# Cross attention: mask widened ahead of the context split, scores issued in pairs on 64 rows each

## The reference, cut to what matters

```
x: 32 x 100 x 256, context: 32 x 361 x 256, mask: 32 x 100 x 361 (bool)
Q = LN(x) Wq + bq;  K = ctx Wk + bk;  V = ctx Wv + bv      16 heads of 16 channels
scores = where(mask, Q K / sqrt(16), lowest float);  A = softmax(scores) V
x = x + tanh(g0) * (A Wo + bo)
x = x + tanh(g1) * experts_attention(LN(x))                8 heads x 8 experts
```

## Time and profile before

| what | value |
|---|---|
| median of 3 runs | 2058.17 us (2057.41 to 2060.99) |
| profiled execution, its own time | 2054.61 us |
| its span, first to last instruction | 2053.0 us |
| busy PE / PEld / DVE / ACT / POOL | 1911.7 / 1177.6 / 1497.5 / 1141.0 / 930.7 us |
| mean granted TensorE clock | 0.970 |

### The profile page before, as it was taken

How to read it: one execution, slowest core, us unless ns; L and a number is a source line. 1 busy time by engine, 2 the same in 40 slices (tenths; PEclk the granted TensorE clock), 3 DMA queues, 4 the chain that set the end, 5 groups by cost and what they waited for, 6 DMA issues and landing times. The chain is left out here.

```text
span 2053.0 us, 59140 instructions
## 1 busy us (share of the span) xinstructions
PE 1911.7 (93%) x13454; PEld 1177.6 (57%) x13454; DVE 1497.5 (73%) x4285; ACT 1141.0 (56%) x3588; POOL 930.7 (45%) x1361
## 2 busy tenths in 40 slices
PE   5788899899889799999999999968999999999998
PEld 2577777777777555444444444436555555555553
DVE  6477777778778795255555555556999999999989
ACT  3477777777778644444444444434555555555543
POOL 3112112211221200266666666653766666767767
PEclk9899999999999899999999999987999999999999
DMA  3676776677666248200000000034222222222201
GB/s 115 120 102 99 103 104 101 104 100 110 100 105 88 82 199 318 124 26 26 26 26 26 26 26 26 26 107 149 83 71 75 76 73 75 71 75 70 84 14 64
DMA packets 192135, 174.07 MB, mean 85 GB/s; under 512 B 51921, under 2 KB 183378, under 8 KB 190034
## 3 DMA queue, kind: packets, MB, share of 16 engines
q1 hardware_dynamic: 189906, 165.06, 35.6%
q0 software_dynamic: 2176, 8.39, 1.2%
HBM read 112.41 MB, written 60.98 MB: 84 GB/s over the span
## 5 line engine op out<-in xcount | busy, mean ns | idle before, releaser
L1343 POOL TENSOR_TENSOR o_side<-o_side,o_tmp 128x256 f32 (+1 forms) x528 | 397.5, 753 | 193.3 <-POOL o_side L1343 73.5
L1069 ACT ACTIVATE big<-e_pv,gates 128x128 f32<-128x128 f32 x800 | 228.0, 368 | 292.1 <-PE e_pv L1131 290.6
L609 ACT ACTIVATE c_ex<-c_sm,c_nmax 100x361 f32<-100x361 f32 x512 | 302.6, 593 | 122.5 <-DVE c_nmax L499 109.6
L499 DVE CUSTOM_DVE_ANT_0 c_sm<-c_ps,c_mbias 100x361 f32<-100x361 f32 x512 | 269.3, 527 | 118.4 <-PE c_ps L687 59.4
L1464 ACT ACTIVATE o_tmp<-o_py,gates 128x256 f32<-128x256 f32 x528 | 221.9, 474 | 192.0 <-PE o_py L1537 141.8
L1131 PE MATMUL e_pv<-e_vhi,e_xhi 128*128 x800 | 303.2, 379 | 1.2 <-ACT e_out L1059 1.2
L1537 PE MATMUL o_py<-o_whi,a_chi 128*128 128x512 f16 x800 | 303.7, 380 | 0.6 <-DVE o_side L1397 0.3
L1131 PE MATMUL e_pv<-e_vlo,e_xhi 128*128 x800 | 303.2, 379 | 0.0
L1131 PE MATMUL e_pv<-e_vhi,e_xlo 128*128 x800 | 303.2, 379 | 0.0
L1537 PE MATMUL o_py<-o_whi,a_clo 128*128 128x512 f16 x800 | 303.1, 379 | 0.0
L1537 PE MATMUL o_py<-o_wlo,a_chi 128*128 128x512 f16 x800 | 303.0, 379 | 0.0
(11 more groups left out here) (166 smaller groups left out, 3401.3 us busy)
## 6 DMA issues: line engine op xcount, KB each, us to landing
qk<-e_out SPq DMA_DIRECT2D x16, 1600.0 KB, 5.2
c_kst<-k_parts SPq DMA_DIRECT2D x256, 90.2 KB, 4.9
v<-e_out SPq DMA_DIRECT2D x20, 640.0 KB, 3.3
a_q<-qk SPq DMA_DIRECT2D x64, 200.0 KB, 2.5
a_k<-qk SPq DMA_DIRECT2D x64, 200.0 KB, 2.4
a_v<-v SPq DMA_DIRECT2D x64, 200.0 KB
c_ctx<-in_ctx_t SPq DMA_DIRECT2D x32, 361.0 KB, 3.4
e_wst<-in_v_w POOLq DMA_DIRECT2D x8, 1024.0 KB, 8.1
```

Of the source, the lines that this page charges most:

```text
L499: dve.tensor_tensor_reduce(out=sm[:, h % 4, :], in0=p_s[0:SQ, h % 2, 0:SK], in1=mbias[:, b.par, :], scale=-0.25 / WS, scalar=BIG, op0=ALU. ...
L609: act.activation(ex[:, h % 4, 0:SK], sm[:, h % 4, :], ACT.Exp, scale=-1.0, bias=nmax[:, h % 4:h % 4 + 1], accum_out=den[:, b.par, HEAD[h]: ...
L1069: act.activation(tmp[:, hh, e, :], p_v[:, hh, 1, e * PD:(e + 1) * PD], ACT.Copy, scale=gate).then_inc(s_av, 1)
L1343: pool.tensor_tensor(side[:, x.t, :], side[:, x.t, :], tmp[:, slot(x, r), j, :], ALU.add).then_inc(s_pool, 1)
```

## The change

It reorders POOL (mask of the next batch ahead of the split, first mask and split ahead of the wait for `s_tg`), gives each scores matmul only the 64 rows that hold its head, issues the scores of two heads together in even steps, reorders `HEAD` so that each two neighbours are an even and an odd head, and lets DVE copy two heads behind every second mask. The accumulation flags of `attend` follow the group of four in place of the parity of the head.

```diff
-HEAD = (0, 2, 4, 6, 1, 3, 5, 7, 8, 10, 12, 14, 9, 11, 13, 15)
+HEAD = (0, 3, 4, 7, 1, 2, 5, 6, 8, 11, 12, 15, 9, 10, 13, 14)
...
-                pool.wait_ge(s_tg, 1)
-
-                def body(b):
+
+                def widen_mask(b):
                     pool.wait_ge(s_mask[b.par], 16 * (b.half + 1))
                     at_least(pool, s_sm, XH * (b.n - 1))
                     pass_wait(pool, s_pass_pool)
                     pool.tensor_scalar(mbias[:, b.par, :], mraw[:, b.par, :], BIG, -BIG,
                                        ALU.mult, ALU.add).then_inc(s_mb, 1)
+
+                def bias_x(b):
                     pool.wait_ge(s_x[b.par], 16 * (b.half + 1))
                     at_least(pool, s_x1, b.n - 1)
                     pool.tensor_tensor(xbias[:, b.par, :], xb[:, b.par, :], tgbo[0:SQ, :],
                                        ALU.add).then_inc(s_xb, 1)
+
+                def body(b):
+                    bias_x(b)
+                    if later(b, 1):
+                        widen_mask(later(b, 1))
                     if later(b, 3):
                         split(later(b, 3))
 
+                widen_mask(fixed(0))
                 split(fixed(2))
+                pool.wait_ge(s_tg, 1)
                 batches(pool, body)
...
                     for i in range(XH):
-                        lagging(b, i, LAG_C, copy_ext)
                         masked(b, i)
+                        if i % 2 == 1:
+                            lagging(b, i, LAG_C, copy_ext)
+                            lagging(b, i, LAG_C - 1, copy_ext)
...
-                for i in range(XH, XH + LAG_C):
-                    lagging(last, i, LAG_C, copy_ext)
+                for h in range(XH - LAG_C + 1, XH):
+                    copy_ext(last, h)
...
-                    pe.matmul(p_s[0:SQ, h % 2, 0:SK], qst[:, b.par, HEAD[h], :], kst[:, b.par, HEAD[h] // 2, :],
+                    row = P // 2 * (HEAD[h] % 2)
+                    pe.matmul(p_s[0:SQ, h % 2, 0:SK], qst[row:row + P // 2, b.par, HEAD[h], :],
+                              kst[row:row + P // 2, b.par, HEAD[h] // 2, :],
                               start=True, stop=True).then_inc(s_s, 1)
...
-                                             start=odd == 0 and c == 0, stop=odd == 1 and c == KC - 1)
+                                             start=first // CLOSE % 2 == 0 and c == 0,
+                                             stop=first // CLOSE % 2 == 1 and c == KC - 1)
...
                     for i in range(XH):
-                        scores(b, i)
+                        if i % 2 == 0:
+                            scores(b, i)
+                            scores(b, i + 1)
```

## The result

| | before | after |
|---|---|---|
| median | 2059.11 us (4 runs, 2057.41 to 2060.99) | 2037.19 us (4 runs, 2034.08 to 2038.59) |
| ratio of the runs | | 0.9891, 95% interval 0.9874 to 0.9908 |
| profiled execution / its span | 2054.61 / 2053.0 us | 2037.69 / 2036.1 us |
| mean granted TensorE clock | 0.970 | 0.976 |

Faster by 22 us (1.1%), where 44 were forecast: the sign was right, the size was half, and the time lies inside the range of 1975 to 2046.

What follows compares the result with a forecast made beforehand. The late mask on POOL was taken to stall DVE and PE, with PE pacing otherwise. Batches go from 18.73 to 16.16 + 0.96 = 17.12 us: 46.7 gained less 2.9, net 43.8, forecast 2014 us, range 1975 to 2046.

Steps and rivals of the forecast that it cites:

- mask ahead of the split: POOL's order: DVE's wait and PE's lowered clock go, 18.73 to 16.16 us per batch, 74.5 us over 29 batches.
- early second score, copies in twos: PE and DVE order within a batch: taken as zero, PE having 2.1 us per pair, DVE needing 1.8.
- halved rows: shape changes less overlap: PE's score pairs: 0.44 us against 0.32 through drains at shape changes, +0.96 us per batch.
- batch 0: First batch: gains no mask wait and pays 0.96 us for its pairs.
- batches 30, 31 and later stages: Last batches: 30 and 31 gain no mask wait and each pay 0.96 us for pairs.
- the 1984 that the prediction has for it: Whole-kernel time in us if a pair of scores costs just what two scores did before.
- The bound that I gave for the late copies alone: DVE's copies of heads 3, 5, 9, 11: at most 4 x 0.464 = 1.86 us per batch on PE's path.
- The second rival: DVE's late copies hold PE: two of four arrive on its path, batch 18.05 us, 2044 us; chance 0.13.
- My own sign of failure: Working fails if PE idles on `c_nmax` or `c_ext` over 1 us per batch: pair cost then does not pace PE.
- The pairs do not gain (1965, 1984): Rival on PE's scores: row halves switch without drain, 1965 us, or pairs cost nothing extra, 1984; chance 0.18.
- the tiles within a pair do not drain against each other (2084): Rival: the lower-to-upper tile step drains too, pair 0.71 us, batch 19.28, 2084 us; chance 0.07.
- The mask does not come last: Rival on the mask's DMA: landing some 5 us after issue, the wait stays, 2058 us; chance 0.06.

Runs made afterwards that it cites:

- mask_only: The kernel before with nothing but POOL's new order (next batch's mask ahead of the split): 1987.4 us, ratio 0.9637.
- pairs_128: The kernel after, but every score multiplies all 128 rows again; order, HEAD and copies as changed: 2007.4 us, ratio 0.9735.
- single_64: mask_only with each score on its own 64 rows, one at a time in the old order: 2092.5 us, ratio 1.0147.
- batch0_128: The kernel after with all 128 rows in batch 0 alone: 2031.1 us, ratio 0.9880.
- pairs_same_rows: The kernel after with the old HEAD list, so both scores of a pair lie on the same 64 rows: 2066.2 us, ratio 1.0010.
- first_64: mask_only with halved rows in batch 0 alone, one score at a time: 1996.3 us, ratio 0.9706.
- pairs_only: The kernel after with POOL's old order: 2148.8 us, ratio 1.0441.

## Why the prediction was right or wrong, point by point

Against the forecast's own base, the profiled execution, the change gave 2054.6 - 2037.7 = 16.9 us and not 43.8. Over the 29 batches from the second to the thirtieth (mean lengths from first mask to first mask; mask_only 16.34, pairs_128 17.15):

| term | forecast us | measured us |
|---|---|---|
| mask ahead of the split | +74.5 | 29 x (18.73 - 16.34) = +69.3 |
| early second score, copies in twos | 0 | 29 x (16.34 - 17.15) = -23.5 |
| halved rows: shape changes less overlap | -27.8 | 29 x (17.15 - 17.77) = -18.0 |
| batch 0 | -1.0 | 15.90 - 23.13 = -7.2 |
| batches 30, 31 and later stages | -1.9 | the rest, -3.7 |

- **Mask.** Right. The wait went, the clock stayed at 1.00 from batch 1 to batch 29, and what came next, PE itself, gave 16.24 to 16.34 us where the unwaited part of a batch at full clock had been 16.16. mask_only landed 3 us from the 1984 that the prediction has for it.
- **Both scores early, copies in twos: "I take zero".** This is the step that failed: 0.81 us a batch, 23.5 of the 26.9 us by which the gain fell short. I compared averages, 2.1 us of PE per pair against 1.8 of DVE, and concluded that PE would find its masks ready. The load within a batch is uneven on both engines. In pairs_128 PE stands at the second score where DVE has a key part between two masks (360.01), and where DVE itself had stood for a transpose (365.36), each time with its transposes queued behind. The bound that I gave for the late copies alone (0 to 1.86 us) holds the 0.6 to 0.7 us that they cost by themselves. The second rival, late copies at +0.93 us a batch and 2044 us, comes nearer to the 2037 measured than my forecast, but in part by luck: its copies alone cost less, the halved rows too cost less than I had added, and the early score and batch 0 were not in it. I gave the early score no bound at all, and it is the dearer half when the copies stay where they were. My own sign of failure was PE standing on `c_nmax` or `c_ext` for more than 1 us a batch. In the kernel after PE itself stands 12.7 / 29 = 0.44 us, its weight loads (20.0 + 11.4) / 29 = 1.08 us, so the sign comes out only if the loads are counted.
- **Halved rows.** Right in kind: entry 0.10 and exit 0.29 as computed from `attend`'s edges, overlap as computed from its inside. The transposes behind pay 0.10, not 0.03. The loads on "issue" are those behind the pair, not those before it as I had expected. Still the batch paid 0.62 us where 0.96 were forecast. Part of it is likely that in pairs like that at 420.37 the second score waits for a mask anyhow; how much is not shown. The rule of the Trainium skill ("TensorEngine Tiling (Array Packing)", section "Tiling Modes": a change of tiling mode drains, a change of tile does not) agrees with both: 0.28 us for one score in single_64, 0.29 for two in the kernel after.
- **The clock.** I had it only as something that the removed wait gives back. Halved rows delay its rise: batch 0 is 7.2 us longer than before, the drains of its own eight pairs included. batch0_128 has batch 0 back at 15.1 us, while its whole time is not clear of that of the kernel after. This was not among the costs or the rivals.
- **The rivals.** The pairs do not gain (1965, 1984), and the tiles within a pair do not drain against each other (2084): both records lie inside 0.36 us. The mask does not come last.

What stays open: why the copies in twos and the early score cost together no more than one of them (the waits show that the transposes' wait for the copies nearly goes, not how the sum comes out), what of the early score's price belongs to the new `HEAD` and flags, and whether the low clock follows from 64 rows as such or from the drains around them. Neither alone can be all of it: pairs_same_rows has the rows and the changes of shape of the kernel after, and its clock rises 27 us later. Between 64-row kernels the stretch is shortest where the two scores run side by side. Behind the last mask the kernels take between 1374 and 1380 us though they share that code; that was not traced.

## What to carry to other kernels

Look first for what a shared in-order engine does ahead of the piece that others wait for. Giving the mask its place ahead of the split on POOL was worth 3.6%, and nothing on PE had to change. A matmul on half of the rows has to pay for the change of shape: here two scores of 0.16 us each do not pay for one change and back. Whether more of them in a row would, no run tried. Where a wait is added to an in-order queue, price it step by step and not on averages, and keep short ready work out from behind it.

## What the runs showed of the hardware that was not expected

- Two 64-row matmuls on opposite halves overlap fully (2 x 353 ns inside 0.36 us), and a pair then takes no more of PE's sequence than one such matmul alone (0.29 and 0.28 us).
- After a stand of PE the granted clock stays at the lower level (1.2 GHz) much longer when the scores use 64 rows. At the start: until about 91 us in mask_only, 108 us in the kernel after, 112 us in single_64, 116 us in first_64 and 135 us with both scores on the same half. single_64 and first_64 run the same batch 0, so some 4 us of such a difference can be chance. The window of pairs_same_rows, 117 to 127 us:

```profile
117.00:127.00 10.00, 10.00 (x60) 7.61 (x60) 5.27 (x19) 4.69 (x16) 0.00 (x0) 0.50 0.95 101
```

- With POOL's old order, under which PE stands at nearly every batch of the kernel before and at every second one of pairs_only, the rest of the change costs 87 us instead of 50.
